# Matrix strips of half a row block, fetched by indirect DMAs over all 128 partitions

## The chip, the core and the metric

The kernel runs on one NeuronCore of a Trainium2 chip. Its engines work beside each other and meet only at semaphores: PE (TensorE) multiplies, DVE (VectorE) and ACT (ScalarE) do elementwise work, POOL (GpSimd) and SP (SyncE) issue DMAs here. Sixteen DMA engines move data between HBM and the on-chip memory SBUF, which has 128 partitions; PE writes its products to PSUM. The metric is the device time of one execution in microseconds (us). Lower is better.

## The reference

`adj` is 8192 x 8192 in float32 (268 MB), not symmetric in its values; `x` is 8192 x 64. Two graph layers are computed, and nearly all of the work is `adj` times a matrix of 64 columns, four times:

```python
h  = relu(layernorm(x))                       # T0
T1 = adj @ h;  T2 = 2*(adj @ T1) - T0;  T3 = 2*(adj @ T2) - T1
x  = x + sum_k(T_k @ w_cheb[k])
h  = relu(layernorm(x))                       # X
deg = clip(sum(adj, axis=1) + 1, 1, None)
z  = concat([h, (adj @ h + h) / deg], axis=1) @ w_sage + b
r  = relu(z)
out = x + r / max(norm(r, axis=1), 1e-12)
```

## The kernel before

**Blocks.** `adj` is cut into 16 x 16 blocks of 512 x 512 elements (1 MB). Row block C holds the rows `a*2048 + c*32 + r` with `c` in 4C..4C+3, and column block J the columns with the same numbering. In SBUF a block has 128 partitions (`a`, 32 rows each) and 16 groups `g` of 128 elements. A *unit* of work is one block: DVE turns its 32 x 32 squares in place (line 601), then PE issues four matmuls of 512 columns (lines 745 and 751). A float32 matmul runs as two instructions on PE, so a block is eight PE instructions.

**Sweeps.** The four products depend on each other, but a block that has been read may serve two of them at once if the second vector is already known: the matmul then has 128 stationary columns (a *pair*, line 745, psum `ps_pair`) instead of 64 (a *single*, line 751, `ps_single`). Sweep 1 reads all 256 blocks row by row and pairs J < C; sweep 2 goes upwards from the last row and reads the upper triangle, where J > C is paired; sweep 3 goes down and reads the lower triangle; sweep 4 reads the upper triangle for the second layer, a part of it (`final=False`) between the rows of sweep 3. Together they read 652 blocks. In sweep 1 the diagonal block of most rows is also kept aside turned (line 597), to be used again one row later (`late_product`).

**Strips and the ring.** A *strip* is up to W = 4 neighbouring blocks of one row block. It is loaded by 32 DMAs: for each row quarter `ar` and each column quarter `a` one DMA writes the 32 partitions of `a`, in rows of up to 4 x 512 B = 2 KB (lines 317 and 351). SP issues those for `a` = 0, 1 (partitions 0 to 63) and POOL those for `a` = 2, 3 (partitions 64 to 127). Strips lie in `ring`, which has 16 places of one block. `ring_places` gives each strip its place, and a strip may be loaded once PE has finished the units of the strips that lay there (`wait_ge(s_unit, ...)`).

**Sums.** The degrees need the sum of each row of `adj`. In sweep 1 ACT goes over every strip before DVE may turn it: 16 ACTIVATE of 512 elements per strip with an accumulated sum (`sum_rows`, line 393). ACT executes in order, and on the same engine stand the copies of PSUM to SBUF: `vec_t` (line 406, waits for PE's transposes of line 642, which PE issues at the third unit of a row), `sum_d` (413), and at the end of a row `sum_s` (420) and `sum_p` (422).

**End of a row.** PE combines `sum_s` and `sum_p` with the weights into `ps_lin` and `ps_tr` (lines 690 to 709), and DVE makes the new rows of `vec`, `res` and `part` of them. The start: SP issues the eight loads of `x` (line 306) and only then its part of the strips, POOL issues strips from the start; DVE and ACT normalise `x` in quarters.

Of the kernel before, what the change touches and what calls it, by code (L numbers as in the profile page):

```python
# [54 lines left out]
W = 4  # L55
SW = NB // W
UC = CB * 32
RING = 16
# [5 lines left out]
STORE_LAG = 6  # L64
# [5 lines left out]
class Row:  # L70


    def __init__(self, sweep, C, strips, final=True):
        self.sweep, self.C, self.strips = sweep, C, strips
        self.final = final
        self.units = [u for _, _, units in strips for u in units]
        self.has_pair = any(kind == PAIR for _, kind in self.units)
        self.has_single = any(kind == SINGLE for _, kind in self.units)
        self.has_late = sweep == 1 and C < LATE_BLOCKS


def sweep_rows():

    rows = []
    for C in range(NB):
        order = [(C // W + 1 + k) % SW for k in range(SW)]
        strips = []
        for s in order:
            Js = list(range(W * s, W * s + W))
            strips.append((Js[0], W, [(J, SINGLE) for J in Js if J >= C] + [(J, PAIR) for J in Js if J < C]))  # L90
        rows.append(Row(1, C, strips))
    for C in reversed(range(NB)):
        strips = []
        first = C + 1 if C < LATE_BLOCKS else C
        for s in reversed(range(first // W, SW)):
            Js = list(range(max(first, W * s), W * s + W))
            units = [(J, PAIR if J > C else SINGLE) for J in reversed(Js)]
            if len(units) > 1 and units[-1][0] == C:
                units[-1], units[-2] = units[-2], units[-1]
            strips.append((Js[0], len(Js), units))  # L100
        rows.append(Row(2, C, strips))
    for C in range(NB):
        strips = []
        for s in range(C // W + 1):
            Js = list(range(W * s, min(C, W * s + W - 1) + 1))
            units = [(J, PAIR if J < C else SINGLE) for J in Js]
            if len(units) > 1 and units[-1][0] == C:
                units[-1], units[-2] = units[-2], units[-1]
            strips.append((Js[0], len(Js), units))
        rows.append(Row(3, C, strips))  # L110

    def upper(C, first, last):

        strips = []
        for s in range(first // W, last // W + 1):
            Js = list(range(max(first, W * s), W * s + W))
            strips.append((Js[0], len(Js), [(J, SINGLE) for J in Js]))
        return strips

    half = NB // 2  # L120
    sweep3, rows = rows[-NB:], rows[:-NB]
    for row in sweep3:
        rows.append(row)


        if W <= row.C < 2 * W:
            C = 2 * W - 1 - row.C
            rows.append(Row(4, C, upper(C, C, W - 1), final=False))
        if row.C >= half:
            C = NB - 1 - row.C  # L130
            rows.append(Row(4, C, upper(C, max(C, W), (half if C >= W else NB - W) - 1), final=False))

    for C in [0, 8, 4, 9, 1, 5, 10, 15, 6, 2, 11, 14, 12, 3, 7, 13]:
        rows.append(Row(4, C, upper(C, max(C, half if C >= W else NB - W), NB - 1)))
    return rows


def ring_places(strips):

    at, places, live = 0, [], []  # L140
    for i, (_, _, w, _) in enumerate(strips):
# [4 lines left out]
        before = max(before, i - NSEM + 1)  # L146
# [6 lines left out]
def cheb_sage_kernel(nc, x, adj, w_cheb, w_sage, b_sage, out):  # L153
    rows = sweep_rows()
    row_index = {(r.sweep, r.C): n for n, r in enumerate(rows) if r.final}
    strips = [(n, J0, w, units) for n, r in enumerate(rows) for J0, w, units in r.strips]
# [10 lines left out]
    def needed_row(row, J, kind):  # L167

        if row.sweep == 1:
            return row_index[1, J] if kind == PAIR else None  # L170
# [613 lines left out]
```

## Time and profile before

| | us |
|---|---|
| runs: 2662.23, 2655.51, 2654.42 | median 2655.51 |
| profiled execution, device time | 2672.75 |
| its span, first to last instruction | 2670.9 |
| row block 0 of sweep 1 done (`sum_s` copied) | 126 |
| sweep 1 done | 1063 |
| sweep 2 done | 1568 |
| sweep 3 with its part of sweep 4 done | 2323 |
| busy PE / DVE / ACT / POOL | 2152.7 / 1637.1 / 730.2 / 821.6 |
| moved by DMA | 689.56 MB, mean 258 GB/s |

The four boundaries are the ends of ACT's copies of lines 420 and 422 for the last row of each stage, rounded to a microsecond. PE's busy time counts each instruction to its modelled end. The share of the DMA engines is the time during which they hold packets, not the rate at which they move them: it can be above 1 when packets of two queues overlap. "PEclk" is the granted clock of TensorE, 1.00 for 2.4 GHz and 0.5 for 1.2 GHz.

### The profile page before, as it was taken

What the parts mean: (1) busy time and instruction counts of PE and PEld (TensorE: products, weight loads), DVE (VectorE), ACT (ScalarE), POOL (GpSimd) and SP (SyncE); (2) the same over time, 40 slices, a digit from 0 to 9 for tenths busy, and PEclk for the clock granted to TensorE, in tenths of its full rate; (3) what the DMA queues carried; (4) which work ended last, traced back from release to release, by engine and by line L of the source; (5) the groups of instructions that cost most, each with busy time, mean ns of one, the idle gap of its engine ahead of it and who ended that gap; (6) DMA issues with size and microseconds to landing.
All of it is one profiled execution on the core that took longest, in us unless ns stands there. A gap on an engine that the chain in (4) does not pass through costs nothing.

```text
span 2670.9 us, 20670 instructions
## 1 busy us (share of the span) xinstructions
PE 2152.7 (81%) x6792; PEld 919.9 (34%) x6792; DVE 1637.1 (61%) x1204; ACT 730.2 (27%) x2243; POOL 821.6 (31%) x1521
## 2 busy tenths in 40 slices
PE   0567778888999999989988979889886897776666
PEld 0123233333334444444434434333332343222222
DVE  2755556656656565756564566766575655576766
ACT  1766666666676674000000000000000000000000
POOL 2222223222322323323222434233232332233423
PEclk9988989999999999999999999889998998888878
DMA  9999999999999999999999999999999999999994
GB/s 206 259 261 265 274 262 268 274 270 268 269 277 276 266 262 258 234 272 238 265 248 259 252 261 257 268 250 269 276 254 268 264 272 267 271 264 270 248 258 127
DMA packets 326445, 689.56 MB, mean 258 GB/s; under 512 B 56514, under 2 KB 93378, under 8 KB 326338
## 3 DMA queue, kind: packets, MB, share of 16 engines
q1 hardware_dynamic: 216832, 344.03, 56.8%
q0 software_dynamic: 108672, 344.03, 46.1%
q8 instruction: 53, 0.87, 0.2%
q14 instruction: 54, 0.44, 0.1%
q10 hardware_dynamic: 834, 0.20, 0.0%
HBM read 685.97 MB, written 2.10 MB: 258 GB/s over the span
## 4 chain that ended last, share of the span: by engine, by line
PE 30%; DMA 29%; SPq 28%; ACT 5%; DVE 5%; issue 2%; POOL 0%; DVEq 0%; ACTq 0%
DMA ring<-in_adj_dram 28%; SPq L317 27%; PE ps_pair L745 23%; ACT ring L393 5%; PE ps_single L751 4%; DVE ring L601 3%; SPq L306 1%; DMA res<-in_x_dram 1%; PE ps_lin L690 0%; PE ps_lin L693 0%; PE ps_lin L706 0%; PE ps_tr L709 0%; PE ps_lin L698 0%; PE ps_xt L642 0%; PE ps_single L652 0%
## 5 line engine op out<-in xcount | busy, mean ns | idle before, releaser
L601 DVE STREAM_TRANSPOSE ring<-ring 128x2048 f32<-128x2048 f32 x640 | 1431.6, 2284 | 810.2 <-DMA ring<-in_adj_dram 536.6
L745 PE MATMUL ps_pair<-ring,vec 128*128 128x512 f32 x2880 | 1319.3, 616 | 151.8 <-DVE ring L601 140.4
L351 POOL DMA_DIRECT2D ring<-in_adj_dram x1448 | 786.0, 551 | 1811.9 <-PE ps_pair L745 1131.1
L745 PEld LDWEIGHTS ps_pair<-ring,vec 128*128 128x128 f32 x2880 | 559.4, 198 | 878.6 <-issue 766.5
L751 PE MATMUL ps_single<-ring,vec 128*64 128x512 f32 x2240 | 591.1, 665 | 285.2 <-DVE ring L601 281.2
L393 ACT ACTIVATE ring<-ring 128x512 f32<-128x512 f32 x1024 | 628.0, 615 | 297.3 <-DMA ring<-in_adj_dram 297.3
L751 PEld LDWEIGHTS ps_single<-ring,vec 128*64 128x64 f32 x2240 | 159.6, 149 | 644.9 <-issue 423.9
L420 ACT ACTIVATE sum_s<-ps_single 128x512 f32<-128x512 f32 x64 | 37.7, 590 | 616.7 <-PE ps_pair L745 449.5
L393 ACT ACTIVATION_READ_ACCUMULATOR ring<-ring 128x1 f32 x1024 | 192.0, 188 | 0.0
L422 ACT ACTIVATE sum_p<-ps_pair 128x512 f32<-128x512 f32 x45 | 26.6, 591 | 452.2 <-PE ps_pair L745 452.2
L431 ACT ACTIVATE stat<-stat 128x4 f32<-128x4 f32 x16 | 3.3, 205 | 258.7 <-DVE stat L554 258.7
L370 ACT ACTIVATE stat<-stat,eps 128x4 f32<-128x4 f32 (+1 forms) x20 | 6.0, 299 | 232.3 <-DVE stat L542 229.9
L597 DVE STREAM_TRANSPOSE vec<-ring 128x512 f32<-128x512 f32 x40 | 25.1, 683 | 72.1 <-ACT ring L393 72.1
L705 PE MATMUL ps_lin<-rhs_x,vec_t 65*128 65x128 f32 x128 | 32.6, 340 | 29.7 <-ACT sum_s L420 29.7
L751 PE MATMUL ps_single<-vec 128*64 128x512 f32 x80 | 25.0, 747 | 28.4 <-DVE vec L597 26.3
L333 POOL DMA_DIRECT2D out_dram<-vec x64 | 34.7, 549 | 26.8 <-DVE vec L570 26.1
L706 PE MATMUL ps_lin<-wb,sum_s 128*128 128x64 f32 x224 | 37.4, 279 | 4.5 <-ACT sum_s L420 4.5
L448 DVE TENSOR_REDUCE stat<-res 128x4 f32<-128x256 f32 (+1 forms) x20 | 11.4, 568 | 46.9 <-DMA res<-in_x_dram 46.9
L706 PEld LDWEIGHTS ps_lin<-wb,sum_s 128*128 128x128 f32 x224 | 35.1, 211 | 13.5 <-ACT sum_s L420 10.4
L705 PEld LDWEIGHTS ps_lin<-rhs_x,vec_t 65*128 65x128 f32 x128 | 22.1, 216 | 45.4 <-ACT sum_s L420 36.6
L690 PE MATMUL ps_lin<-rhs_s,sum_s 128*128 128x128 f32 x128 | 33.3, 345 | 1.2 <-ACT sum_p L422 1.2
L693 PE MATMUL ps_lin<-rhs_x,vec_t 64*128 64x64 f32 x128 | 29.7, 315 | 0.0
(95 smaller groups left out, 576.7 us busy)
## 6 DMA issues: line engine op xcount, KB each, us to landing
ring<-in_adj_dram POOLq DMA_DIRECT2D x1160, 256.0 KB, 12.1
ring<-in_adj_dram SPq DMA_DIRECT2D x1160, 256.0 KB, 18.4
ring<-in_adj_dram POOLq DMA_DIRECT2D x96, 192.0 KB, 11.2
ring<-in_adj_dram SPq DMA_DIRECT2D x96, 192.0 KB, 18.6
ring<-in_adj_dram POOLq DMA_DIRECT2D x96, 128.0 KB, 10.9
ring<-in_adj_dram SPq DMA_DIRECT2D x96, 128.0 KB, 13.9
ring<-in_adj_dram SPq DMA_DIRECT2D x96, 64.0 KB, 15.2
ring<-in_adj_dram POOLq DMA_DIRECT2D x96, 64.0 KB, 10.2
```

Source lines behind the costliest of these rows:

```text
L317: sp.dma_start(dst, src).then_inc(s_low[i % NSEM], 16)
L333: pool.dma_start(out_v[a, :, CB * C:CB * C + CB, :], vec[32 * a:32 * a + 32, CB * C:CB * C + CB, 0, :]).then_inc(s_out, 16)
L351: pool.dma_start(dst, src).then_inc(s_high[i % NSEM], 16)
L393: last = nc.scalar.activation(strip_of(i)[:, g, :], strip_of(i)[:, g, :], ACT.Copy, accum_out=strip_sums[:, C % 2, J0 // W, g:g + 1])
L420: last = nc.scalar.activation(sum_s[:], ps_single[n % 2][:], ACT.Copy)
L601: nc.vector.transpose(blocks, blocks).then_inc(s_turned, 1)
L690: nc.tensor.matmul(both, S, rhs_s1[:], start=True, stop=False)
L693: last = nc.tensor.matmul(lin, XT[0:F, :], rhs_x1[:], start=False, stop=True)
L705: nc.tensor.matmul(both, XT, rhs_x4[:], start=True, stop=False)
L706: last = nc.tensor.matmul(lin, S, wb[:], start=not row.final, stop=True)
L745: last = nc.tensor.matmul(ps_pair[n % 2][:], vec[:, CB * J + c, :, :], moving, start=(k == pair_at[0] and c == 0), stop=(k == pair_at[-1] ...
L751: last = nc.tensor.matmul(ps_single[n % 2][half:half + F, :], vec[:, CB * J + c, single_slot, :], moving, start=(k == single_at[0] and c < 2),
```

## The change

- **Strips** are now half a row block high (H = 2; `h` says which half: 8 of the 16 groups `g`) and up to WIDE = 12 blocks wide. The ring has 32 places of half a block, the same bytes. In sweep 1 a row block is four strips of 8 places; in the triangles a row block is two strips as wide as the row, or four. `ring_places` now also never lets a strip be released earlier than the one before it.
- **Loads.** Strips of 4 or more places are loaded by POOL alone: 8 indirect DMAs each, one per group, which take one row of up to 12 x 512 B = 6 KB for each of the 128 partitions by a table `index`. There are 168 such strips, 1344 DMAs, 1244 places of 512 KB. The 30 strips of 1 to 3 places (60 places) are loaded by SP as before, 16 DMAs each. SP also stores the results.
- **Units** are now up to GROUP = 2 neighbouring half-blocks: one transpose of the same 2048 elements, and eight matmuls of 256 columns instead of four of 512. There are 680 units. Within a row those that hold the newest row's block or the diagonal come last, of both halves (`early + behind`), so both strips in which they lie are complete only with the last two units of the row.
- **Sums.** In sweep 1 only the half of the columns that doesn't hold C is summed, in 16 ACTIVATE of 1024 elements per row block; the rest is summed in sweeps 2 and 3 when it is read again, and DVE adds it to `row_sums`. A strip that is summed is still summed before it is turned. `sum_rows` is called by unit number.
- **Start.** `x` is loaded by SP and ACT, four DMAs each, and POOL waits for all of it before it issues the first strip.

```diff
@@ sizes
-W = 4
-RING = 16
-STORE_LAG = 6
+H = 2
+GH = G // H
+RING = 32
+WIDE = 12
+GROUP = 2
+NARROW = 3
+STORE_LAG = 12
+SUM_LEAD = 4
@@ class Row
+        for k, (_, J0, w) in enumerate(pieces):
+            groups = [list(range(J, min(J + GROUP, J0 + w))) for J in range(J0, J0 + w, GROUP)]
+            for Js in (reversed(groups) if sweep == 2 else groups):
+                (behind if latest in Js or self.has_late and C in Js else early).append((k, Js))
+        self.units = early + behind
@@ sweep_rows
+def split(first, last):
+    n = last - first + 1
+    parts = -(-n // WIDE)
...
@@ ring_places
-        before = max(before, i - NSEM + 1)
+        before = max(before, i - NSEM + 1, places[-1][1] if places else 0)
@@ release of a strip
+    free_at = [max(strip_done[:before], default=0) for _, before in places]
@@ pool
+            for h in range(2):
+                pool.wait_ge(s_x[h], 16 * Q)
+            for i in wide_strips:
+                n, h, J0, w = strips[i]
+                if free_at[i] > 0:
+                    pool.wait_ge(s_unit, free_at[i])
+                for g in range(GH):
+                    at = CB * rows[n].C + CB // H * h + g // Q
+                    pool.indirect_dma_start(
+                        strip_of(i)[:, g, :], None, adj_q,
+                        bass.IndirectOffsetOnAxis(ap=index[:, 0:1], axis=0),
+                        element_offset=(QN * (g % Q) + 32 * at) * N + J0 * UC)\
+                        .then_inc(s_wide[wide_strips.index(i) % NSEM], 16)
@@ scalar, once per row
+                sum_rows(row_start[n] + SUM_LEAD)
                 if n in x_rows:
...
                 if n - 1 in late_at:
+                    sum_rows(late_at[n - 1] + SUM_LEAD)
...
-                if n + 1 < len(rows):
-                    sum_rows(first_strip[n + 1])
+                sum_rows(row_start[n + 1] + 1)
                 act.wait_ge(s_unit, row_start[n + 1])
```

How ACT's work of a row block in sweep 1 (C = 1) is ordered before: one strip of 16 sums, `vec_t`, two more strips, `sum_d`, the first strip of the next row block, then the copies of the row's sums.

```order
L393 ACTIVATE ring,strip_sums<-ring 128x512 x16
L406 ACTIVATE vec_t<-ps_xt 64x512
L393 ACTIVATE ring,strip_sums<-ring 128x512 x32
L413 ACTIVATE sum_d<-ps_single 128x512
L393 ACTIVATE ring,strip_sums<-ring 128x512 x16
L420 ACTIVATE sum_s<-ps_single 128x512
L422 ACTIVATE sum_p<-ps_pair 128x512
```

And now, for the same row block, with lines of the changed file: one strip of 8 sums between `vec_t` and `sum_d`, and one, which belongs to the next row block, between `sum_d` and the copies.

```order
L454 ACTIVATE vec_t<-ps_xt 64x512
L443 ACTIVATE ring,row_sums<-ring 128x1024 x8
L460 ACTIVATE sum_d<-ps_single 128x512
L443 ACTIVATE ring,row_sums<-ring 128x1024 x8
L466 ACTIVATE sum_s<-ps_single 128x512
L468 ACTIVATE sum_p<-ps_pair 128x512
```

So the second strip of a row block is summed behind `vec_t`, and the first strip of the next one ahead of `sum_s`.

POOL's loads in sweep 2 before, rows C = 15 down to 10: half of each strip, in rows of at most 512 elements.

```order
L351 DMA ring<-in_adj_dram 32x4x128 x8
L351 DMA ring<-in_adj_dram 32x4x256 x8
L351 DMA ring<-in_adj_dram 32x4x384 x8
L351 DMA ring<-in_adj_dram 32x4x512 x24
L351 DMA ring<-in_adj_dram 32x4x128 x8
```

And now, the rows C = 8 to C = 2 of that sweep: whole rows of 7, 8, 9, 10, 11 and 12 places, two strips of eight DMAs each, and then the first two strips of the row C = 2.

```order
L395 DMA ring<-in_adj_dram,index 128x896 x16
L395 DMA ring<-in_adj_dram,index 128x1024 x16
L395 DMA ring<-in_adj_dram,index 128x1152 x16
L395 DMA ring<-in_adj_dram,index 128x1280 x16
L395 DMA ring<-in_adj_dram,index 128x1408 x16
L395 DMA ring<-in_adj_dram,index 128x1536 x16
L395 DMA ring<-in_adj_dram,index 128x896 x16
```

Two strips of 11 or 12 places fill 22 or 24 of the ring's 32 places, so the next strip of that width goes to a place that is held until the row before is complete.

## Rows read from the trace of the kernel before

**Rows 1.** The page: busy time, share of the span, instructions; slices; DMA queues.
```profile
PE 2152.7 (81%) x6792; PEld 919.9 (34%) x6792; DVE 1637.1 (61%) x1204; ACT 730.2 (27%) x2243; POOL 821.6 (31%) x1521
...
DMA  9999999999999999999999999999999999999994
GB/s 206 259 261 265 274 262 268 274 270 268 269 277 276 266 262 258 234 272 238 265 248 259 252 261 257 268 250 269 276 254 268 264 272 267 271 264 270 248 258 127
...
q1 hardware_dynamic: 216832, 344.03, 56.8%
q0 software_dynamic: 108672, 344.03, 46.1%
```

**Rows 2.** Stretches of 5 us: length, busy engines (instructions), clock, DMA share, GB/s.
```profile
60.00:65.00 5.00, 0.00 (x0) 0.00 (x0) 4.97 (x6) 1.47 (x3) 0.00 (x0) 1.00 1.07 203
65.00:70.00 5.00, 0.00 (x0) 0.00 (x0) 4.70 (x15) 5.00 (x17) 0.00 (x0) 1.00 1.07 200
...
110.00:115.00 5.00, 4.49 (x22) 1.26 (x20) 5.00 (x3) 0.00 (x0) 0.85 (x2) 1.00 1.04 301
```

**Rows 3.** The timeline of POOL, then of SP, from the start.
```profile
2.10 17.49 POOL L351 DMA_DIRECT2D ring<-in_adj_dram  x32 [0.32 <-issue]
87.21 4.34 POOL L351 DMA_DIRECT2D ring<-in_adj_dram  x8 [67.62 <-PE ps_single L751]
...
46.10 31.16 SPq L317 DMA_DIRECT2D ring<-in_adj_dram  x32
```

**Rows 4.** Groups of instructions: line, engine, operation, count, busy, mean ns, idle before.
```profile
L601 DVE STREAM_TRANSPOSE ring<-ring 128x2048 f32<-128x2048 f32 x640 | 1431.6, 2284 | 810.2 <-DMA ring<-in_adj_dram 536.6
L351 POOL DMA_DIRECT2D ring<-in_adj_dram x1448 | 786.0, 551 | 1811.9 <-PE ps_pair L745 1131.1
L393 ACT ACTIVATE ring<-ring 128x512 f32<-128x512 f32 x1024 | 628.0, 615 | 297.3 <-DMA ring<-in_adj_dram 297.3
L393 ACT ACTIVATION_READ_ACCUMULATOR ring<-ring 128x1 f32 x1024 | 192.0, 188 | 0.0
```

**Rows 5.** The timeline of PE: pairs, transposes with full weights, singles.
```profile
1103.76 7.13 PE L745 MATMUL ps_pair<-ring,vec 128*128 128x512 f32 x16
...
1168.34 0.61 PE L709 MATMUL ps_tr<-ident,sum_p 128*128 128x128 f32 x4
...
271.43 8.99 PE L751 MATMUL ps_single<-ring,vec 128*64 128x512 f32 x40
```

**Rows 6.** The five stages of the table, columns as in Rows 2.
```profile
0.00:126.00 126.00, 32.56 (x132) 8.81 (x132) 59.50 (x63) 57.88 (x172) 35.87 (x73) 0.98 1.06 229
126.00:1063.00 937.00, 798.39 (x2580) 336.90 (x2580) 569.78 (x372) 613.29 (x1946) 261.29 (x482) 0.93 1.05 268
1063.00:1568.00 505.00, 463.45 (x1220) 214.16 (x1220) 296.09 (x177) 11.13 (x20) 159.88 (x295) 0.96 1.02 254
1568.00:2323.00 755.00, 629.50 (x1852) 269.22 (x1852) 469.08 (x345) 27.42 (x59) 238.77 (x440) 0.92 1.06 265
2323.00:2671.00 348.00, 228.75 (x1008) 90.84 (x1008) 242.67 (x247) 20.46 (x49) 125.80 (x232) 0.83 0.95 234
```

**Rows 7.** The chain that ended last, at the start: from, length, what.
```profile
5.92 16.19 SPq L306
22.15 16.13 SPq L306
38.32 15.00 DMA res<-in_x_dram
53.34 1.23 DVE stat L448
...
65.10 6.26 ACT ring L393 x21
```

**Rows 8.** Two views: SP's waits in the timeline of SP; PE's wait in sweep 2.
```profile
904.59 20.24 SPq L317 DMA_DIRECT2D ring<-in_adj_dram  x10
...
1197.76 6.61 PE L745 MATMUL ps_pair<-ring,vec 128*128 128x512 f32 x8 [8.21 <-DVE ring L601]
```

More of the change, by code:

```diff
@@ L85, in sweep_rows @@
     for C in range(NB):
[L86 to L91, printed above, removed]
+        runs = [(0, NB // 2), (NB // 2, NB // 2)]
+        if C and C - 1 < NB // 2:
+            runs.reverse()
+        rows.append(Row(1, C, [(h, J0, w) for J0, w in runs for h in range(H)], C - 1))
@@ L112, in upper @@
[L112 to L131, printed above, removed]
+        runs = split(first, NB - 1)
@@ new lines, in sweep_rows, with upper @@
+        rows.append(Row(2, C, [(h, J0, w) for J0, w in reversed(runs) for h in range(H)], C + 1))
+    def upper(C, first, last):
+        return [(h, J0, w) for J0, w in split(first, last) for h in range(H)]
+    half, W = NB // 2, NB // 4
+    for C in range(NB):
+        rows.append(Row(3, C, [(h, J0, w) for J0, w in split(0, C) for h in range(H)], C - 1))
+        if W <= C < 2 * W:
+            D = 2 * W - 1 - C
+            rows.append(Row(4, D, upper(D, D, W - 1), None, final=False))
+        if C >= half:
+            D = NB - 1 - C
+            rows.append(Row(4, D, upper(D, max(D, W), (half if D >= W else NB - W) - 1), None, final=False))
@@ L133, in sweep_rows @@
     for C in [0, 8, 4, 9, 1, 5, 10, 15, 6, 2, 11, 14, 12, 3, 7, 13]:
-        rows.append(Row(4, C, upper(C, max(C, half if C >= W else NB - W), NB - 1)))
+        rows.append(Row(4, C, upper(C, max(C, half if C >= W else NB - W), NB - 1), None))
     return rows
@@ L140, in ring_places @@
     at, places, live = 0, [], []
-    for i, (_, _, w, _) in enumerate(strips):
+    for i, (_, _, _, w) in enumerate(strips):
         if at + w > RING:
@@ new lines, in _ @@
+            finished = sorted((n, C) for (sweep, C), n in row_index.items() if sweep == 4)
+            stored = 0
+            for i in narrow_strips:
+                n, h, J0, w = strips[i]
+                while stored < len(finished) and begin_at[finished[stored][0]] + STORE_LAG < free_at[i]:
+                    store_row(*finished[stored])
+                    stored += 1
+                if free_at[i] > 0:
+                    sp.wait_ge(s_unit, free_at[i])
+                at = CB * rows[n].C + CB // H * h
@@ L714, in _ @@
             for n, row in enumerate(rows):
-                pair_at = [k for k, (_, kind) in enumerate(row.units) if kind == PAIR]
-                single_at = [k for k, (_, kind) in enumerate(row.units) if kind == SINGLE]
+                pairs = sum(CB for _, Js in row.units for J in Js if row.kind(J) == PAIR)
+                singles = sum(CB for _, Js in row.units for J in Js if row.kind(J) == SINGLE)
+                pair, single = 0, 0
                 single_slot = {1: 0, 2: 1, 3: 0, 4: 1}[row.sweep]
```

322 lines of the change are left out of this document (167 added, 155 removed).

## The prediction, made before the changed kernel was run

> **What bounds the kernel now.** I read the page first. The DMA engines hold packets in all 40 slices while the rate stays between 206 and 277 GB/s, and PE is busy for 81% of the span, DVE for 61% [rows 1]. So the transfers bound it, with PE close behind. The second view is the stretches of 5 us, to see what the "full" DMA engines do. From 60 to 70 us only SP's half of the strips is moving: POOL had issued its 32 DMAs by 19.6 us and issues nothing until 87.2, SP issues from 46.1 to 77.3 [rows 3]. In that stretch the share is 1.07 and the rate 203 and 200 GB/s; from 110 to 115 us, with both halves on their way, the share is 1.04 and the rate 301 [rows 2]. The engines are equally occupied and move half as much again, so a packet waits for its destination: 64 partitions take about 200 GB/s, and two streams that meet at random take up to 301, on average 258. The third view is PE's timeline: pairs start every 0.43 us (7.13 us for 16, with a tail), singles cost 0.22 us each (8.99 us for 40) [rows 5]. A block is eight instructions, hence 3.44 us as a pair and 1.8 us as singles, against 4.1 us of transfer at 258 GB/s. The last view is the five stages of the table: PE is idle for 93, 139, 42, 126 and 119 us in them [rows 6], 518 us in all. That is what a faster transfer can win back, and no more than that, if PE's own work stays.
>
> **PE and DVE, the same work in other pieces.** 256 columns instead of 512 halve each instruction and double their number, with the weights loaded twice as often. The transposes with full weights and only 128 columns follow each other every 0.11 us (0.61 us for 4 with the tail) [rows 5], so a weight load of 128 columns already hides behind a quarter of the old matmul; it will hide behind half of it. I take 0; the bounds are 0, since no instruction does more work, and +16 us, if each of the 5200 added instructions costs the 3 ns by which 0.11 us exceeds a quarter of 0.43. DVE turns 2048 elements in 2.28 us as before [rows 4]; 28 more units, of half size, cost some 30 us of DVE, which has room.
>
> **The rate.** A DMA over all partitions reaches both halves at once. Lower end 258 GB/s (today's mean, if the limit is on the reading side), upper end 406 (twice the 203 of one half). I take 390, near the upper end, because the row at 203 is a direct measurement of one half with the engines full. A place (512 KB) then takes 1.34 us, a strip of 8 places 10.8 us, one of 12 places 16.1.
>
> The Trainium skill, "SBUF — State Buffer", section on Door 1, the port swizzle, says that 64 partitions reach only half of the 16 ports; by that the 203 GB/s is explained, and the trace agrees. The same notes, "DMA: Bandwidth & Descriptors", section "Where 436 GB/s comes from", speak against a gain of this size: for HBM to SBUF about 358 GB/s bind. No row here shows that limit, since none of the stretches in rows 2 goes above 301. By it the loads would take 9% longer than I assume and the sum below would be about 27 us more.
>
> **POOL's issue.** The trace has no indirect DMA. A plain one of 128 pieces holds POOL for 0.551 us [rows 4]: that is the lower end, since the indirect one writes as many and must read 128 indices besides. The only longer hold of a queue in the trace is SP's, 2.02 us for each DMA when it is pushed back (20.24 us for 10) [rows 8]: the upper end. I take 1.1 us, twice the plain one and nearer to it. A DMA of 8 places' width carries 512 KB and needs 1.34 us of transfer, so POOL is hidden there; at 4 places (256 KB) POOL limits to 238 GB/s.
>
> **Stage by stage.**
> - *Row block 0: 126 -> 112.* The chain shows `x` landing at 53.3 us and 12 us of normalising behind it [rows 7], while POOL's first 32 DMAs are under way [rows 3]. Alone, its 2 MB need 10 us at 203 GB/s; for their small rows I take 17. Then four strips of 10.8 us arrive until 61 plus landing, two of them are summed (8 x (1.04 + 0.19) = 9.8 us each, scaled from 615 and 188 ns [rows 4]) and PE is through at about 90. But ACT's copy of the row's sum now stands behind the sum of the next row's first strip, which is released only with the last units of row 0: 90 + 10.8 + 9.8 + 1 = 112.
> - *Rows 1 to 15 of sweep 1: 937 -> 920.* PE's work is 798 us [rows 6]. In each row the second strip is summed behind `vec_t`, that is after PE's third unit; 9.8 us of sums and 2.3 us of DVE stand against PE's two remaining units of the first strip, 3.4 us (singles) in rows 1 to 8 and 6.9 us (pairs) in rows 9 to 15: waits of 8.7 x 8 + 5.2 x 7 = 106 us. Another 15 us at row ends. The sum on ACT falls from 64 x 0.8 = 51 us a row to 19.7, but the wait is one of order, not of load.
> - *Sweep 2: 505 -> 560.* PE works 463.5 us. Both strips of a row are complete only with its last units, and strips of 11 and 12 places don't fit three times into 32 places. The strip for C = 3 is released by the last unit of the row before: 16.1 us of load, 5 of landing, hand-over and first transpose, nothing under it: 21 us idle, where today's wait for a turned block is 8.21 us [rows 8]. The one for C = 4 has one unit of cover: 14.8 + 5 - 3.4 = 16. Those for C = 5 and 6 have 17 and 15.5 us of cover, 3 us idle together; C = 0, where four loads queue up, about 10. With the 42 us of today's idle time, which at this rate are mostly the dependencies at row ends [rows 6], 463.5 + 50 + 42 = 556, and 4 for POOL's pace at 4 places.
> - *Sweep 3 with its part of sweep 4: 755 -> 805.* PE works 629.5. The same collision at C = 8 to 11: 12.1 + 5 - 6.9 = 10 and 5 for its second strip; 3; 14.8 + 5 - 6 = 14 and 4; 16.1 + 5 - 8.6 = 12.5 and 8; later rows 8: 65 us. Of today's 126 us of idle time I keep 110: in rows of one to eight places each row waits for the one before, whatever the rate.
> - *The last rows: 348 -> 285.* 84 blocks. The 20 in strips of 4 places take 80 x 1.1 = 88 us by POOL, the other 64 take 67 MB / 390 = 172 us: 260, with PE at 229 and DVE at 243 beside it [rows 6], and 25 for the start and the final row.
>
> The sum is 112 + 920 + 560 + 805 + 285 = 2682, against a span of 2670.9. The profiled execution took 1.9 us more than its span (2672.75) and the median of the runs was 17.2 us under that, so I expect 2682 + 1.9 - 17.2 = 2667 us. What the faster transfer wins at the start and the end, the ring and ACT's order lose in between.
>
> **Rivals.**
> 1. *The transfer is worth more than I allow.* At 406 GB/s with the plain issue price of 0.55 the last stage is bound by DVE (260), sweep 3 takes 775, sweep 2 540 and sweep 1 905; with 110 for row 0 this is 2590, a median of 2575. For it: PE's 518 us of idle time are large, and 5 us of landing may be 3. Against it: the strips of 11 and 12 places are released too late at any rate.
> 2. *POOL becomes the bound* (slower; it decides from about 1.4 us per indirect DMA). At 1.6 us a strip takes 12.8 us however narrow. The last stage has 26 such strips, 333 us plus 25 instead of 285: +70; in the short rows of sweeps 2 and 3, where PE needs 14 to 18 us for two strips of 25.6, another +30: about 2770. At the upper end, 2.02 us, 1344 DMAs are 2715 us of issue alone, over 2780. Against it: only the unproven price.
> 3. *The limit is on the reading side* (slower). At 300 GB/s the last stage's 88 MB take 293 instead of 226 us (+40 with POOL's part unchanged), the exposed loads of sweeps 2 and 3 grow by a third (+45), sweep 1 by 15 and row 0 by 10: about 2780. Against it: equal shares at 203 and 301 GB/s.
>
> **How the numbers follow.** The forecast 0.46, rival 1 0.27, rival 2 0.17, rival 3 0.10. A measurement of this kernel can tell 0.3% (8 us) from no change: faster is below 2647.5, slower above 2663.5. The forecast's own range is 2630 to 2715; of its 0.46, 0.09 lie below, 0.10 within and 0.27 above. With rival 1 faster gets 0.36, with rivals 2 and 3 slower gets 0.54. The predicted time is the forecast's, 2667. The range reaches to rival 1 and to rivals 2 and 3: 2575 to 2790.
>
> **What would show it.** Right: stretches at 380 GB/s or more in sweep 1; PE waiting for DVE, and DVE for a DMA, about 20 us before C = 3 of sweep 2 and before the widest rows of sweep 3; in each row of sweep 1 one wait of PE of 5 to 9 us that ends with ACT's sum; DMA shares falling well below 1. Wrong: POOL's DMAs of 1.4 us and more; a rate that stays near 300 with the engines full (rival 3); a sweep 2 shorter than today's (then my reading of the ring is wrong); pair instructions more than 0.22 us apart in an unbroken run (then the weight loads show).

## The result and the profile after

| | us |
|---|---|
| changed kernel, four runs, median (lowest to highest) | 2688.06 (2684.29 to 2691.95) |
| kernel before, four runs beside it | 2654.97 (2653.15 to 2662.23) |
| ratio, 95% interval | 1.012 (1.0094 to 1.0145) |
| profiled execution, its span | 2684.29, 2682.5 |

The change makes the kernel 1.2% slower, a small loss that is clear of the interval. The forecast was 2667. The page of the changed kernel, beside [rows 1]:

```profile
PE 2150.1 (80%) x12008; PEld 1661.5 (62%) x12008; DVE 1637.2 (61%) x1306; ACT 678.8 (25%) x1667; POOL 1268.9 (47%) x1357
...
DMA  9699889668877766965467777667655989989995
GB/s 284 218 329 326 301 288 315 231 225 280 286 272 254 252 219 168 302 207 217 172 243 259 233 221 209 200 203 253 222 198 173 336 287 360 332 260 354 365 272 162
...
q0 software_dynamic: 163840, 652.30, 71.3%
q1 hardware_dynamic: 51776, 34.64, 4.9%
```

The DMA engines, full in every slice before, now stand at 4 to 9 tenths, and the rate of a slice runs from 162 to 365 GB/s: the path is faster where it works and waits elsewhere. PE is busy for the same time (2150.1 after, 2152.7 before).

The five stages, from the windows of the trace; columns as in [rows 2], boundaries taken as in [rows 6]:

```profile
0.00:117.00 117.00, 34.43 (x260) 19.97 (x260) 60.49 (x69) 34.35 (x60) 52.20 (x67) 0.85 0.77 237
117.00:1029.00 912.00, 784.81 (x4501) 589.81 (x4501) 564.45 (x412) 274.61 (x523) 429.89 (x459) 0.93 0.79 271
1029.00:1594.00 565.00, 471.45 (x2212) 403.01 (x2212) 297.64 (x199) 152.25 (x483) 241.69 (x256) 0.93 0.69 231
1594.00:2385.00 791.00, 634.74 (x3368) 502.54 (x3370) 475.68 (x378) 197.75 (x556) 362.29 (x384) 0.91 0.75 250
2385.00:2682.00 297.00, 224.69 (x1672) 146.18 (x1668) 238.96 (x250) 19.83 (x48) 182.88 (x193) 0.86 0.89 293
```

| stage | before | forecast | after | PE idle before / after |
|---|---|---|---|---|
| row block 0 | 126 | 112 | 117 | 93 / 83 |
| rows 1 to 15 of sweep 1 | 937 | 920 | 912 | 139 / 127 |
| sweep 2 | 505 | 560 | 565 | 42 / 94 |
| sweep 3 with its part of 4 | 755 | 805 | 791 | 126 / 156 |
| last rows | 348 | 285 | 297 | 119 / 72 |
| sum | 2671 | 2682 | 2682 | 519 / 532 |

The start and the last rows gained 60 us and sweep 1 another 25, and sweeps 2 and 3 gave back 96.

How fast the path can be, in stretches of 5 us; the first of row block 1, the other two while PE waits in sweep 2:

```profile
155.00:160.00 5.00, 4.26 (x36) 2.30 (x36) 5.00 (x4) 5.00 (x11) 3.75 (x4) 1.00 1.02 384
...
1305.00:1310.00 5.00, 1.49 (x4) 1.25 (x5) 2.88 (x2) 2.50 (x9) 0.00 (x0) 0.50 1.02 421
...
1365.00:1370.00 5.00, 0.00 (x0) 0.00 (x0) 0.00 (x0) 0.00 (x0) 3.78 (x5) 0.50 1.02 424
```

With full engines (share 1.02) the path moves 421 and 424 GB/s where it moved 203 and 301 before [rows 2]. These are the best stretches: over all windows of 5 us with a share of 1.00 or more the median is 359 GB/s now (424 the highest), against 279 (316 the highest) in the kernel before. In the last two rows PE does next to nothing, at a granted clock of 0.50 (1.2 GHz): full transfer and idle PE stand side by side.

POOL's issue: first its group (columns as in [rows 4]), then two DMAs in a row of its timeline.

```profile
L395 POOL DMA_INDIRECT ring<-in_adj_dram,index x1344 | 1267.4, 943 | 1356.4 <-PE ps_single L806 503.2
...
1285.47 0.93 POOL L395 DMA_INDIRECT ring<-in_adj_dram,index  x1 [0.30 <-issue]
1286.71 0.93 POOL L395 DMA_INDIRECT ring<-in_adj_dram,index  x1 [0.30 <-issue]
```

POOL is held for 0.943 us and begins the next 0.30 us later: one indirect DMA per 1.24 us.

The two places where the prediction put new waits. PE in row block 2 of sweep 1 and ACT in front of it:

```profile
178.20 3.67 PE L806 MATMUL ps_single<-ring,vec 128*64 128x256 f32 x32
189.68 5.51 PE L806 MATMUL ps_single<-ring,vec 128*64 128x256 f32 x32 [7.80 <-DVE ring L652]
...
178.31 0.59 ACT L454 ACTIVATE vec_t<-ps_xt 64x512 f32<-64x512 f32 x1 [8.09 <-PE ps_xt L694]
178.80 1.04 ACT L443 ACTIVATE ring<-ring 128x1024 f32<-128x1024 f32 x1
...
186.07 1.04 ACT L443 ACTIVATE ring<-ring 128x1024 f32<-128x1024 f32 x1
...
187.31 4.50 DVE L652 STREAM_TRANSPOSE ring<-ring 128x2048 f32<-128x2048 f32 x2 [11.38 <-ACT ring L443]
```

ACT copies `vec_t` at 178.3 and only then sums the second strip, eight times, until 187.2; DVE turns it, PE goes on at 189.68. Such a wait is 7.8 us in each of the rows 1 to 8 and 4.5 us in each of the rows 9 to 15, 94 us in all. Sweep 1 has one longer wait, at the start of row 9:

```profile
585.57 4.71 PE L800 MATMUL ps_pair<-ring,vec 128*128 128x256 f32 x12 [18.70 <-DVE ring L652]
```

POOL begins to issue this strip at 557.4, once PE has finished the unit that frees its places; the strip has landed at 574.6, ACT has summed it at 583.0 and DVE turned a unit at 585.4. That is the wait for a late strip which the prediction has only in sweeps 2 and 3.

And PE in sweep 2, at the starts of the rows C = 4 and C = 3, with the chain of waits (start, length, what) through the second:

```profile
1308.51 3.75 PE L800 MATMUL ps_pair<-ring,vec 128*128 128x256 f32 x8 [21.10 <-DVE ring L652]
...
1313.80 36.43 PE L800 MATMUL ps_pair<-ring,vec 128*128 128x256 f32 x168
1378.13 5.25 PE L800 MATMUL ps_pair<-ring,vec 128*128 128x256 f32 x16 [27.91 <-DVE ring L652]
...
1350.50 0.93 POOL ring L395
...
1359.19 11.35 DMA ring<-in_adj_dram,index
1370.54 0.02 issue
1370.56 1.38 ACT ring L443 x5
...
1375.67 2.32 DVE ring L652
```

PE's last unit of C = 4 ends at 1350.24. It releases the strip, POOL issues its eight DMAs from 1350.50, the eighth is issued at 1359.19 and lands at 1370.54, ACT sums until 1375.6, DVE turns a unit, and PE goes on 27.9 us after its last unit. No work of PE lies under it.

### The profile page after: what moved, and what is told of

Its sections match the earlier page's. It is cut to its first block, busy times and chain, and to the rows that moved or that the text cites. A ratio compares the mean times of both kernels' runs of the same rounds, so it can differ in the third digit from the quotient of the medians.

```text
span 2682.5 us, 29450 instructions
## 1 busy us (share of the span) xinstructions
PE 2150.1 (80%) x12008; PEld 1661.5 (62%) x12008; DVE 1637.2 (61%) x1306; ACT 678.8 (25%) x1667; POOL 1268.9 (47%) x1357
## 4 chain that ended last, share of the span: by engine, by line
PE 44%; POOL 18%; ACT 11%; DMA 10%; DVE 9%; issue 9%; ACTq 0%; POOLq 0%; DVEq 0%
PE ps_pair L800 32%; POOL ring L395 18%; ACT ring L443 11%; DMA ring<-in_adj_dram,index 9%; DVE ring L652 7%; PE ps_single L806 7%; PE ps_lin L742 1%; PE ps_lin L745 1%; PE ps_single L704 1%; PE ps_tr L761 0%; DMA res<-in_x_dram 0%; PE ps_late L715 0%; PE ps_lin L744 0%; ACT vec_t L454 0%; PE ps_xt L694 0%
## 5 line engine op out<-in xcount | busy, mean ns | idle before, releaser
L652 DVE STREAM_TRANSPOSE ring<-ring 128x2048 f32<-128x2048 f32 (+1 forms) x680 | 1430.8, 2155 | 887.9 <-ACT ring L443 714.7
L395 POOL DMA_INDIRECT ring<-in_adj_dram,index x1344 | 1267.4, 943 | 1356.4 <-PE ps_single L806 503.2
L800 PE MATMUL ps_pair<-ring,vec 128*128 128x256 f32 x5760 | 1349.1, 395 | 258.6 <-DVE ring L652 243.6
L800 PEld LDWEIGHTS ps_pair<-ring,vec 128*128 128x128 f32 x5760 | 1128.4, 198 | 466.9 <-issue 142.1
L806 PE MATMUL ps_single<-ring,vec 128*64 128x256 f32 x4480 | 575.4, 408 | 237.5 <-DVE ring L652 230.4
L443 ACT ACTIVATE ring<-ring 128x1024 f32<-128x1024 f32 (+7 forms) x736 | 574.6, 784 | 590.3 <-DMA ring<-in_adj_dram,index 569.1
L806 PEld LDWEIGHTS ps_single<-ring,vec 128*64 128x64 f32 x4480 | 329.5, 146 | 454.0 <-DVE ring L652 181.7
L443 ACT ACTIVATION_READ_ACCUMULATOR ring<-ring 128x1 f32 x736 | 138.7, 188 | 0.0
L454 ACT ACTIVATE vec_t<-ps_xt 64x512 f32<-64x512 f32 x32 | 18.7, 583 | 172.2 <-PE ps_xt L694 172.2
L647 DVE STREAM_TRANSPOSE vec<-ring 128x256 f32<-128x256 f32 x80 | 27.9, 403 | 0.0
```

Of the source, the lines that this page charges most:

```text
L395: pool.indirect_dma_start(strip_of(i)[:, g, :], None, adj_q, bass.IndirectOffsetOnAxis(ap=index[:, 0:1], axis=0), element_offset=(QN * (g ...
L443: last = nc.scalar.activation(cells, cells, ACT.Copy, accum_out=into[:, GH * h + g:GH * h + g + 1])
L647: last = nc.vector.transpose(dst.rearrange("p k (e r) -> p k e r", e=2), src)
L652: last = nc.vector.transpose(blocks, blocks)
L800: last = nc.tensor.matmul(ps_pair[n % 2][:, cells], vec[:, CB * J + c, :, :], moving, start=(pair == 0), stop=(pair == pairs - 1))
L806: last = nc.tensor.matmul(ps_single[n % 2][side:side + F, cells], vec[:, CB * J + c, single_slot, :], moving, start=(single < 2), stop=(si ...
```

## The experiments

Each changes the changed kernel, except `x_first`. They ran in four groups on different chips (the first four together, the next four, the next three, the last alone), each beside the kernel before, so only ratios are compared between groups.

**First group.** `wide8` replaces WIDE = 12 by 8. `act_order` lets one call of `sum_rows` in each of the rows 1 to 15 of sweep 1 reach one unit further, so that the second strip is summed ahead of `vec_t`:

```diff
-                sum_rows(row_start[n] + SUM_LEAD)
+                sum_rows(row_start[n] + (SUM_LEAD + 1 if row.sweep == 1 and n else SUM_LEAD))
```

`short_sums` lets each of the eight sums of a strip cover 32 elements only (its degrees leave out the rest). `direct` loads the wide strips without indirect DMAs:

```diff
+                    for a in ((0, 2, 1, 3) if narrow[i] else (0, 1)):        # SP
...
-                for g in range(GH):
-                    pool.indirect_dma_start(strip_of(i)[:, g, :], ...)
+                for ar in range(Q):
+                    for a in (2, 3):
+                        pool.dma_start(strip_of(i)[32 * a:32 * a + 32, ar:GH:Q, :], ...)
```

> The changed kernel with WIDE = 8 instead of 12, nothing else: rows of more than 8 places become four strips. Theory (the wide strips are released too late, the ring is the loss in sweeps 2 and 3): the waits before C = 5, 4, 3 of sweep 2 and C = 8 to 11 of sweep 3 go, sweep 1 stays at 1029 us, sweep 2 gets 50 to 60 us shorter (565 to about 510), sweep 3 with its part of sweep 4 some 80 us shorter, in all about 2545 us. Rival A (PE pays for matmuls of 256 columns): no change, 2688. Rival B (POOL's 1.24 us per indirect DMA is the bound): slower, since 22 strips of 9 to 12 places become 44, that is 176 DMAs more, 218 us of issue, up to 2800.

> The changed kernel with one number changed in sweep 1: ACT sums the second strip of a row ahead of the copy vec_t, not behind it. Theory (a wait of order, not of load): PE's wait of 5 to 9 us in each of rows 1 to 15 of sweep 1 goes, sweep 1 ends 105 to 120 us earlier (1029 to about 915), the stages behind it keep their lengths, about 2575 us. Rival A (256 columns) and rival B (POOL's pace): sweep 1 keeps its length, 2688. Rival C (ACT's load of sums, not their place, holds sweep 1): under 30 us.

> The changed kernel in which each sum on ACT covers 32 elements of its row only (the degrees leave out the rest): 1.23 us becomes about 0.41, the places of the sums stay. Theory: what PE waits for in sweep 1 is 8 sums that start after its third unit; 9.8 us become 3.3, so the waits of 5 to 9 us shrink to about 0 to 2 and the 9.8 us at the end of row block 0 as well: sweep 1 ends at about 900, in all about 2470 to 2540 us, and most of it in sweep 1. Rivals A and B: no change.

> The changed kernel with the same strips, units and sums, but the wide strips loaded as before by direct DMAs of 32 partitions, half by SP (partitions 0 to 63), half by POOL (64 to 127), in rows of up to 6 KB. Theory (the number of partitions that a DMA reaches sets the rate): the rate falls back to about 260 to 300 GB/s in spite of the long rows, the DMA share goes to 1.0, and the exposed loads get longer: 2820 to 3000 us. Rival D (long rows alone make the rate): the rate stays over 340 GB/s and the time at 2690. Rival B (POOL's indirect issue is the bound): faster than 2650, since a direct DMA holds POOL for 0.55 us.

The stages are those of the table above; the last one ends here with the last copy of `sum_s`, about 10 us before the end of the span.

| | median | ratio to before | stages |
|---|---|---|---|
| wide8 | 3007.93 | 1.1305 (1.1252 to 1.1357) | 118, 1052, 611, 894, 315 |
| act_order | 2942.77 | 1.1052 (1.1002 to 1.1102) | 118, 959, 624, 902, 326 |
| short_sums | 2898.28 | 1.0879 (1.0819 to 1.0938) | 105, 963, 600, 888, 329 |
| direct | 2911.95 | 1.0927 (1.0881 to 1.0973) | 125, 932, 634, 875, 336 |

The theory of each of the first three is missed by 350 us and more and their rivals by 200 and more, and in stages that the edit doesn't touch: `wide8` has the changed kernel's sweep 1, word for word, and takes 1052 us there instead of 912. The traces show what is new. PE in `act_order`, and POOL beside it:

```profile
188.30 0.38 PE L806 MATMUL ps_single<-ring,vec 128*64 128x256 f32 x1 [1.53 <-issue]
189.01 0.51 PE L806 MATMUL ps_single<-ring,vec 128*64 128x256 f32 x1 [0.34 <-issue]
191.11 1.30 PE L806 MATMUL ps_single<-ring,vec 128*64 128x256 f32 x2 [1.58 <-issue]
193.90 1.39 PE L806 MATMUL ps_single<-ring,vec 128*64 128x256 f32 x2 [1.50 <-issue]
...
189.11 0.94 POOL L395 DMA_INDIRECT ring<-in_adj_dram,index  x1 [0.31 <-issue]
190.36 0.94 POOL L395 DMA_INDIRECT ring<-in_adj_dram,index  x1 [0.30 <-issue]
```

PE's instructions come 0.70, 1.40 or 2.10 us apart, in steps of 0.70, within one unit, whose matmuls wait for nothing after the first; POOL keeps its pace. The window from 188 to 197 us, columns as in [rows 2]:

```profile
188.00:197.00 9.00, 4.04 (x9) 1.38 (x9) 3.94 (x3) 0.00 (x0) 4.57 (x5) 0.56 1.02 396
```

The path is full (396 GB/s) and TensorE's granted clock is 0.56, mostly its lower level. Counted over the starts of PE's matmuls and weight loads (at least three such distances, each within 0.03 us of a step and less than 8 us apart) there are 38 stretches of 402 us in `act_order`, 49 of 443 in `wide8`, 39 of 400 in `short_sums`, none in `direct`, in the kernel before and in the changed kernel. So three of the four say nothing of their edits until the stretches are explained.

`direct` has none and stands, inside its theory's range (2820 to 3000): with 32 partitions per DMA the same strips, order and matmuls cost 9% against before instead of 1%. In its windows of 5 us with a share of 1.00 or more the median is 290 GB/s and the highest 340, so the long rows alone don't make the rate (rival D), and POOL's shorter issue of 0.53 us doesn't make it faster (rival B). Against the control below it loses 5 us in row block 0, 16 in rows 1 to 15 of sweep 1, where ACT's order bounds, 70 in sweep 2, at a mean of 206 GB/s there instead of 232, 83 in sweep 3 with its part of sweep 4 and 50 in the last rows.

**Second group.** The changed kernel as a control (`after_again`), `act_order` repeated, and two new ones. `x_first` gives the kernel before the new start (`x` by SP and ACT, both wait for it ahead of the strips). `sum_ahead_8`:

```diff
-WIDE = 12
-GROUP = 2
+WIDE = 8
+GROUP = 1
...
-                sum_rows(row_start[n] + SUM_LEAD)
+                sum_rows(row_start[n] + (9 if row.sweep == 1 and n else SUM_LEAD))
```

> The changed kernel once more, unaltered, as the control that the four runs before lacked. They were 210 to 320 us slower than the changed kernel, and in three of them (the ones with indirect DMAs) the trace shows stretches in which TensorE's instructions start 0.70, 1.40 or 2.10 us apart while SBUF data are there and the wait is put down to issue: 38 stretches of 402 us in all in the run with the sum one unit later, 49 of 443 us in the run with wide strips of 8 KB's limit, 39 of 400 us in the run with short sums, none in the trace of the changed kernel and none in the run with direct DMAs. Theory A (the loss belongs to the chip on which a kernel with indirect DMAs ran, not to the edits): on a chip where the control is slow, it comes out at about 2688 + 250 to 400 = 2940 to 3090 us, with such stretches in sweep 1 once a row; on a chip where it is not, 2688 us within 10 and no such stretch. Theory B (the edits bring it, by where their instructions lie): 2688 us here, while the run of the sum one unit later, repeated beside it, stays at 2940. The two are told apart by the pair.

> The run with the sum of the second strip one unit later in sweep 1, repeated on the chip of the control. Theory A: it differs from the control by its own mechanism alone. The trace of the changed kernel has, per row of sweep 1, one wait of 7.8 us of TensorE that ends with ScalarE's sum; rows 1 to 15 have 15 of them, so with them gone the time is lower than the control's by up to 15 x 7.8 = 117 us: 2570 us if the control is 2688, and in a control with the stretches lower by less, since the stretches stand in the same places as those waits, by 0 to 117. Theory B: 2940 us beside a control of 2688.

> The kernel before with one part of the change alone: the input x is loaded first, by the queues of SyncE and ScalarE, and the first adjacency loads of both queues wait for it. In the kernel before row block 0 ends at 126 us and in the changed kernel at 117. If that is the gain of x coming first, this kernel is 5 to 12 us faster than before. Rival: row block 0 gained by the 6 KB rows and the higher rate, and loading x first only delays the first strips by the 2.1 MB of x at 300 GB/s, 7 us: 0 to 7 us slower than before.

> The changed kernel with three numbers altered: strips of up to 8 places where it has 12 (a new strip then needs 8 free places and not 12), one strip of a row loaded at a time (GROUP 1 for 2), and in sweep 1 the row sums of a strip 9 units ahead of their strip's first use. Theory A on a chip without the stretches: the waits before wide strips in sweeps 2 and 3 (18.6, 21.0, 27.8, 14.4, 19.7, 20.3 us and smaller ones, 451 us of waits over 2.5 us in all) fall to about a third and the waits for ScalarE in sweep 1 go: 2688 - 117 - 150 to 200 = 2370 to 2420 us. On a chip with the stretches about 400 us more. Theory B: nothing is known of the stretches here; the run of the 8 place strips before took 3008 us, and this one would be 2890 to 3010.

| | median | ratio to before | stages |
|---|---|---|---|
| after_again | 2686.25 | 1.0093 (1.0064 to 1.0121) | 120, 916, 563, 792, 286 to the last row |
| act_order_again | 2597.41 | 0.9755 (0.9711 to 0.9799) | 117, 825, 565, 794, 286 |
| x_first | 2645.82 | 0.9931 (0.9905 to 0.9956) | 111, 939, 501, 757, 322 |
| sum_ahead_8 | 2422.04 | 0.9098 (0.9053 to 0.9143) | 116, 820, 495, 702, 277 |

None of the four traces has a stretch. The pair decides between theories A and B: the same program, `act_order`, takes 2943 us on one chip and 2597 on the other, and the kernel before 2663 on both. The unaltered changed kernel never ran on a chip with stretches. PE's waits (for what, us in all, times, longest) in the first and in the second run of it:

```profile
PE ps_single L806 <- issue: 181.2, 150, 26.0
PE ps_pair L800 <- issue: 164.1, 81, 28.2
PE ps_pair L800 <- DVE ring L652: 96.8, 18, 20.5
```

```profile
PE ps_pair L800 <- DVE ring L652: 212.6, 45, 27.4
PE ps_single L806 <- DVE ring L652: 192.0, 50, 40.1
...
PE ps_single L806 <- issue: 4.7, 3, 1.7
```

So the stretches come with the place where the kernel ran and not with the edit alone. What they are isn't shown.

The traces hold one more difference, which makes the recording itself a rival: each of the six traces with stretches lacks nearly half of its semaphore records (18,260 in the first run of `act_order`, 32,911 in the second, with the same 29,450 instructions), and no trace without stretches does. The time from the profiler may therefore contain a hold of the recorder, and every execution on record has a span and a granted clock, so none is known to have run unrecorded. It also makes "issue" in these traces a weak word: it stands wherever no releasing record was found. Two simpler causes don't fit. The loads of the program's own instructions are alike in both runs (94 loads of 16 KB, median 0.96 and 0.97 us), and a full path alone doesn't hold PE up: in the second run PE is busy for over 90% in 58 of the 106 windows of 5 us that move 370 GB/s or more.

What can be concluded here:

- *The order of ACT's sum* is worth 91 us (916 to 825 in rows 1 to 15; elsewhere within 3). PE has the same row without its wait, 80 instructions in one piece:

```profile
182.52 8.85 PE L806 MATMUL ps_single<-ring,vec 128*64 128x256 f32 x80
```

- *x first* is worth 17 us in the kernel before, 15 of them in row block 0 (126 to 111), more than my 5 to 12; the rival (a delay) is out. The changed kernel ends that block at 117 to 120, so the strips and sums take back what `x` gives.
- *Narrower strips and units of one half-block,* with the sum's order of `act_order`, take 264 us off the control and 175 off `act_order_again`. The two traces differ by 178: 5 in rows 1 to 15 of sweep 1, 70 in sweep 2, 92 in sweep 3 with its part of sweep 4, 9 in the last rows, the rest in row block 0. Sweep 2 falls to 495 and sweep 3 to 702, less than before the change (505, 755). The expectations of this run and of `group1` say that GROUP = 1 makes POOL load strips one at a time; it doesn't. POOL issues one strip after the other in both kernels, and GROUP sets how many half-blocks DVE turns and PE waits for as one unit. PE now does the row C = 4, whose first unit came after a wait of 21 us in the changed kernel, in one piece:

```profile
1188.81 1.00 PE L750 MATMUL ps_lin<-rhs_p,sum_p 128*128 128x64 f32 x8
1189.64 0.61 PE L761 MATMUL ps_tr<-ident,sum_p 128*128 128x128 f32 x4
1190.09 38.25 PE L800 MATMUL ps_pair<-ring,vec 128*128 128x256 f32 x176
```

From there to 1403 us no wait of PE is longer than 2.5 us. This is the fastest version, 9% faster than before, and the only one that is faster than before in every stage. The 18.7 us ahead of row 9 in sweep 1 are still there, 21.8 now.

**Third group**, to divide those 175 us between WIDE and GROUP, and to repeat `short_sums`. `group1` is GROUP = 1 alone.

> One number altered, as in the run of this edit before (WIDE 8 for 12): a new strip of the wide rows waits for 8 free places of the ring and not 12, its DMAs stay 128 rows each. That run fell where TensorE's instructions came 0.70 us apart in 49 stretches of 443 us; the control run has since shown that such stretches come with the chip the run is on. Theory (the long waits of sweeps 2 and 3 are the time to free and fill a wide strip): sweep 1, whose strips have at most 8 places in both kernels, stays at 1036 us within 5; sweep 2 falls from 563 us to 505 to 515 (the waits of 20.7 and 27.5 us at 1295 and 1357 fall to a third); the stage of sweep 3 with part of sweep 4 falls from about 795 to 715; in all 2543 to 2560 us. Rival (the first, unrepeated reading: a strip of 8 places is moved less well, because each DMA is a third shorter and POOL pays 1.24 us for each): sweep 2 no shorter than 563 us and the whole 2690 us or more.

> One number altered (GROUP 1 for 2): the loads of the two wide strips of a row block are issued one after the other, each as soon as its places are free, where the changed kernel issues them as a pair. Theory: in sweep 1 the second strip's issue no longer delays the first, which takes about 5 us a row off: sweep 1 ends at 955 to 965 us instead of 1036, sweep 2 is 555 us, the whole 2574 to 2600 us. Rival (the pair is there so that SyncE's and POOL's halves balance, and without it POOL waits at each strip): 2690 to 2750 us.

> Every row sum on ScalarE covers 32 elements of its strip instead of all, so that a sum takes a fraction of its time (the row sums are then those of part of the row). All else is as in the changed kernel. Theory: the 7.8 us waits of TensorE for ScalarE's sum in each row of sweep 1 go as with the sum one unit later (then 2686 fell to 2597), and the waits of VectorE for ScalarE fall too, so the time is 2500 to 2540 us. Rival (the wait is for the order alone: a sum that is short but in the same place still waits for its own strip to land): 2640 us or more.

They came out at 3027.18 (1.1412, 1.1353 to 1.1471), 3007.53 (1.1332, 1.127 to 1.1395) and 2914.60 (1.0979, 1.0906 to 1.1051), with 47 stretches of 501 us, 37 of 337 and 36 of 421. All three miss, and neither theory nor rival can be read from them. Taking the stretches off is no way out: for `act_order` it gives 2943 - 402 = 2541 where the clean run took 2597. How much of the 175 us is WIDE's and how much GROUP's was not measured.

Which of the two frees the ring can be worked out, from the order of units and `ring_places` in the kernels: it gives the work that PE still has between the unit that releases a strip and the strip's first unit, at 0.217 us per pair instruction and half of that per single. For the first strips of C = 4 and C = 3 in sweep 2 that is 3.5 and 0 us with WIDE = 12, 1.7 and 0 with GROUP = 1 beside it, and at least 22 us with WIDE = 8, whatever GROUP is. So the waits of 21 and 28 us are WIDE's by this estimate. For the first strip of row 9 in sweep 1 it is 8.7 us with GROUP = 2 and 4.3 with GROUP = 1, at either WIDE, in keeping with the waits of 18.7 and 21.8 us.

What the runs of this group do show is that the stretches are reproducible: `wide8` had 49 and 47 on two chips, at nearly the same places.

**Last.** In rows 1 to 15 of sweep 1 most stretches begin 12 to 16 us into a run of 16 indirect DMAs, when on average some 5 are in flight (issued by POOL, completion not yet written), and end about 3 us after POOL's last. The runs without stretches have as many in flight, up to 11. So `paced` is `sum_ahead_8` with at most four in flight:

```diff
+                    k, pair = divmod(wide_strips.index(i) * 4 + g // 2 - 2, 4)
+                    if g % 2 == 0 and k >= 0:
+                        pool.wait_ge(s_wide[k % NSEM][pair], 32 * (k // NSEM + 1))
```

> The kernel of the run sum_ahead_8 (2422 us, without stretches) with POOL held back: each wide strip's eight indirect DMAs count on four semaphores of two each, and POOL issues a pair only when the pair two before has landed, so at most 4 indirect DMAs are in flight, where up to 11 were. ScalarE and VectorE wait for the four semaphores. In the slow runs the stretches with TensorE's instructions 0.70 us apart start in sweep 1 when 5.0 to 5.6 indirect DMAs are in flight, about 13 us into a run of 16 of them, and end about 3 us after POOL's last. Theory C (many indirect DMAs in flight bring the stretches where they come at all): on a chip that shows them, no or few stretches, and the time is 2422 plus what the holding back costs, 0 to 120 us: 2425 to 2540. Rival D (they come with the indirect DMAs as such, or with the chip alone, whatever is in flight): on such a chip 2422 + 300 to 450 + 0 to 120 = 2750 to 2990 us with 30 or more stretches. On a chip without stretches both give 2425 to 2540 us and C stays open; the run then says only what holding back costs.

It took 2911.82 us (1.0958, 1.0914 to 1.1001), above the range of theory C and inside D's, but with no stretch, which D excludes. Both fail on the price of holding back: 490 us over `sum_ahead_8`, where both allowed 0 to 120. PE's and POOL's groups of it:

```profile
L805 PE MATMUL ps_pair<-ring,vec 128*128 128x256 f32 x5760 | 1396.6, 404 | 317.5 <-DVE ring L657 305.3 <-DVE vec L507 10.0 <-DVE vec L581 1.4
L398 POOL DMA_INDIRECT ring<-in_adj_dram,index x1472 | 1387.4, 943 | 1482.5 <-DMA ring<-in_adj_dram,index 854.7 <-issue 273.7 <-PE ps_single L811 185.3
```

POOL waits 855 us for its own DMAs, and rows 1 to 15 of sweep 1 run at 262 GB/s instead of the 302 of `sum_ahead_8` (951 us against 820). Four DMAs in flight don't fill the path. Whether this chip would have shown stretches isn't known, since no control ran beside it: theory C stays open.

## Why the prediction came out as it did

- *What bounds.* Right. The rate at full engines rose from 203 and 301 to 421 and 424 GB/s, and `direct`, with 32 partitions per DMA, falls back to a median of 290 with full engines: how many partitions a DMA reaches was the limit. I took 390 and gave 406 as the upper end. Both are low for the best stretches and high for the usual ones (median 359 with full engines): the strip for C = 3 had landed 20.3 us after its release, where I had 16.1 and a share of the 5 us for the landing. The Trainium skill, "DMA: Bandwidth & Descriptors", section "Where 436 GB/s comes from", had 358 GB/s binding; the trace goes against that for this core alone, with 424. The section "Measured" of the same page of the Trainium skill gives 425 for large transfers of a single core, with the other core of the pair idle, and 358 with both streaming; the trace agrees with the first, and no run here shows the second.
- *256 columns for nothing.* Right: 168 pair instructions in 36.43 us, 0.217 us each, against 0.43 for twice the columns [rows 5]. DVE's large form takes 2.280 us in the trace, 2.284 before.
- *POOL's issue.* Taken at 1.1 us; it is 1.24 from one to the next. Rival 2 needed 1.4 and is out. An 8-place DMA (0.524 MB) is therefore limited by POOL to 422 GB/s, just under what the path does, so rival 1's rate was reached without its price.
- *Row block 0.* 117 for 112. `x` landed at 14.2 us, not 17, and POOL issued the next row's strip at 90.8, as said (90). From there it took 26 us to the end and not 22: I had counted its transfer (10.8) and its sums (9.8). The strip had landed after 17.2 us, POOL's eight issues and the landing of the last, and the sums took 8.4.
- *Sweep 1, ACT's order.* The mechanism was right and `act_order_again` shows it: 91 us for the 106 of the prediction (the waits are 7.8 us in rows 1 to 8 where I had 8.7, and 4.5 in rows 9 to 15 where I had 5.2). The price of a sum was too high: ACT starts one every 1.04 us, its read of the accumulator lies under the next one, so eight take 8.4 us and not 9.8; in the kernel before they start every 0.61 us and not 0.80. It was called a wait of order and not of load; that it goes with the order alone, at equal load, is shown. The 18.7 us ahead of row 9 I didn't foresee; the 15 us for row ends happened to cover most of them.
- *Sweep 2.* 565 for 560, and the waits are where they were put, but sized wrongly one by one: 27.9 us at C = 3 (predicted 21), 21.1 at C = 4 (predicted 16), and 3.9 and 4.9 at C = 6 and 5 (predicted 3 together). The chain says what the terms left out: ACT's sum of these strips, 4 to 5 us ahead of DVE. It counted for nothing in the total because the 10 us for C = 0 (the longest wait there is 3.7) and other idle time came out lower. A sum that fits by cancelling isn't a confirmation of its terms.
- *Sweep 3.* 791 for 805: I kept 110 us of today's idle time and added 65; 156 are left. The three longest waits of the stage are 14.5, 19.8 and 20.3 us, again longer one by one than predicted (14 at most).
- *Last rows.* 297 for 285, at 293 GB/s. At 1.24 us POOL takes 80 x 0.14 = 11 us more for the narrow strips than I had, which would be the difference; no run took it alone.
- *From the span to the median.* This is the step that was off. The stages add up to 2682 as predicted, in part by luck: their errors of +5, -8, +5, -14 and +12 us cancel. But I took off 17.2 us, since the profiled execution before had been that much above its median. The changed kernel's was 3.8 below its own. Of the 21 us between forecast and result this is all; one profiled execution's distance from the median belongs to that execution and isn't carried to another kernel.
- *The rivals.* None came. Rival 1 had the rate right (424 over 406) and was wrong about its worth: PE's idle time went from 519 to 532 us. Where the time went: ACT's order holds 91 us, by a run that changes nothing else; strips of up to 12 places and units of two half-blocks hold 175 together, and only the reckoning of the release says that the ring's part is WIDE's.

## What to carry to other kernels

A faster path is worth only what the buffers let it run ahead. When what is loaded together grows from a quarter of the ring to three quarters, the load becomes a step between two units instead of something under them; look at the ratio of the largest piece to the ring before looking at the rate. And on an engine that executes in order, a short job behind a late one costs as much as the late one: place it by the time at which its input is ready. Run an unaltered control beside every group of experiments: without it three runs of the first group here would have told a wrong story.

## What was not expected of the hardware

- The path to all 128 partitions moved 421 and 424 GB/s with rows of 5.5 and 6 KB per partition, and an indirect DMA of 128 rows took POOL 1.24 us from one to the next, from 4 to 12 places wide (0.93 us at the least and 0.94 in the median for its own time).
- Kernels with indirect DMAs showed, in six runs on two chips, stretches in which PE's instructions came in steps of 0.70 us, 337 to 501 us in all, and were 9 to 14% slower than before; four runs of such kernels elsewhere, of a program among them that had 38 here, had none. POOL's pace was unchanged in them, and neither the kernels without indirect DMAs nor the one with four in flight had any. Nearly half of the semaphore records are missing from exactly these six traces. What differs between the places, whether the number in flight is the cause, and whether the recording is, was not found.
- With at most four indirect DMAs in flight the path gave 262 GB/s in rows 1 to 15 of sweep 1, with up to eleven 302.
